# First batch of a two-layer LoRA kernel: another order of VectorE's work around `u_sum`, `h` and the turns of x

## The reference

```
x = x + x @ W0.T + 0.5 * (x @ A0[label]) @ B0.T
x = x + x @ W1.T + bias + 2 * (x @ A1[slot]) @ B1[slot]
```

## Time and profile before

| | |
|---|---|
| timed runs, median (lowest to highest) | 310.39 us (309.81 to 310.56) |
| profiled execution, its own time | 311.65 us |
| its span | 309.8 us |
| mean granted TensorE clock | 0.994 |
| TensorE matmul busy | 300.8 us (97%), 1397 instructions |
| VectorE busy | 233.0 us (75%), 314 |
| ScalarE busy | 139.6 us (45%), 223 |
| GpSimd busy | 68.1 us (22%), 80 |

### The profile page before, as it was taken

How to read it: one execution, slowest core, us unless ns; L and a number is a source line. 1 busy time by engine, 2 the same in 40 slices (tenths; PEclk the granted TensorE clock), 3 DMA queues, 4 the chain that set the end, 5 groups by cost and what they waited for, 6 DMA issues and landing times.

```text
span 309.8 us, 4337 instructions
## 1 busy us (share of the span) xinstructions
PE 300.8 (97%) x1397; PEld 246.1 (79%) x1397; DVE 233.0 (75%) x314; ACT 139.6 (45%) x223; POOL 68.1 (22%) x80
## 2 busy tenths in 40 slices
PE   5999999999999999889999999999999999999995
PEld 4887888888888888578888878878878878878874
DVE  2468997989999999973975975876876876876221
ACT  3556566889348643334254244245245245245010
POOL 4706000010010501520080080080080070070000
PEclk9999999999999999979999999999999999999999
DMA  5999410800006300462283183183093084002012
GB/s 181 293 326 315 49 24 3 129 8 2 0 0 110 62 0 1 65 140 85 37 158 104 29 149 118 22 155 118 16 162 112 17 152 132 11 34 102 0 47 90
DMA packets 99362, 27.55 MB, mean 89 GB/s; under 512 B 84885, under 2 KB 93077, under 8 KB 99350
## 3 DMA queue, kind: packets, MB, share of 16 engines
q1 hardware_dynamic: 99350, 27.41, 37.9%
HBM read 19.01 MB, written 8.39 MB: 88 GB/s over the span
## 4 chain that ended last, share of the span: by engine, by line
PE 79%; DVE 14%; issue 4%; DMA 2%; SPq 0%; ACT 0%; DVEq 0%
PE bank L1026 76%; DVE vt_lo L633 3%; PE bank L1048 2%; DVE xt L855 2%; DVE vt L633 2%; DMA n<-in_L_cond_W 2%; DVE v_lo L633 1%; DVE lhs_lo L633 1%; DVE v L633 1%; DVE s_sum L633 1%; DVE s_lo L633 1%; DVE u_sum L633 0%; DVE z_sum L633 0%; DVE p_lo L633 0%; DVE c_lo L633 0%
## 5 line engine op out<-in xcount | busy, mean ns | idle before, releaser
L1026 PE MATMUL bank<-vt_hi,s_hi 128*128 128x512 f32 x96 | 37.4, 390 | 0.0
L1026 PE MATMUL bank<-vt_lo,s_hi 128*128 128x512 f32 x96 | 37.4, 390 | 0.0
L1026 PE MATMUL bank<-vt_hi,s_lo 128*128 128x512 f32 x96 | 37.3, 389 | 0.0
L855 DVE STREAM_TRANSPOSE xt<-raw 128x512 int32<-128x512 int32 x32 | 32.4, 1082 | 0.0
L417 ACT ACTIVATE lhs_hi<-xt 128x512 fp32r<-128x512 f32 x32 | 19.8, 630 | 25.5 <-PE bank L1026 17.8
L633 DVE TENSOR_TENSOR s_lo<-s_sum,s_hi 128x512 fp32r<-128x512 f32 x32 | 27.6, 886 | 2.9 <-ACT s_hi L417 2.9
L633 DVE TENSOR_TENSOR lhs_lo<-xt,lhs_hi 128x512 fp32r<-128x512 f32 x32 | 24.5, 772 | 4.4 <-ACT lhs_hi L417 4.1
L417 ACT ACTIVATE s_hi<-s_sum 128x512 fp32r<-128x512 f32 x32 | 19.7, 629 | 17.2 <-PE bank L1026 11.0
L377 POOL CAST ac<-c_hi 128x128 fp32r (+1 forms) x8 | 5.7, 707 | 95.1 <-PE bank L1026 86.3
L1026 PE MATMUL bank<-v_lo,lhs_hi 128*128 128x512 f32 x64 | 25.8, 404 | 0.0
L1026 PE MATMUL bank<-v_hi,lhs_lo 128*128 128x512 f32 x64 | 25.0, 391 | 0.0
(11 more groups left out here) (166 smaller groups left out, 753.9 us busy)
## 6 DMA issues: line engine op xcount, KB each, us to landing
raw<-in_x SPq DMA_DIRECT2D x32, 256.0 KB, 4.8
out<-y SPq DMA_DIRECT2D x32, 256.0 KB, 2.1
n<-in_L_cond_W SPq DMA_DIRECT2D x16, 256.0 KB, 6.0
a<-in_L_cond_W SPq DMA_DIRECT2D x16, 256.0 KB, 5.3
a_raw<-in_L_cond_lora_A SPq DMA_DIRECT2D x8, 128.0 KB, 2.4
a_raw<-in_L_cond_lora_As SPq DMA_DIRECT2D x8, 64.0 KB, 2.4
b_raw<-in_L_cond_lora_Bs SPq DMA_DIRECT2D x8, 64.0 KB, 2.0
b_raw<-in_L_cond_lora_B_w SPq DMA_DIRECT2D x1, 128.0 KB, 6.3
```

The costliest lines, as they stand in the source:

```text
L855: nc.vector.transpose(xt[:, n, :, :].rearrange("p e (s sb) -> p sb e s", sb=GR).bitcast(I32), rows[:, n // 2, n % 2].bitcast(I32)).then_in ...
L1026: return nc.tensor.matmul(ps, lhsT, rhs, start=start, stop=stop, skip_group_check=more)
```

## The change

In batch 0 alone VectorE works in another order. Of vt4's four low parts, which stood ahead of the batch, two now stand between `u2_sum` and `u_total`, two behind `u_total`. Quarters 0 and 1 of the next x are turned next; then `z_sum`; then quarter 2; then `h`, which waits for the correction; then z2; then u's low part; then quarter 3, and the low parts of quarter 0, A0 and quarter 2, which stood ahead of and behind `z_sum`. What follows (the low part of sum 0, of quarter 1, the output additions) stays. In the other batches the order is the same as before; `h_and_low` is cut into two functions that stand one behind the other there.

```diff
-            def h_and_low(b):
+            def h_sum(b):
                 dve.wait_ge(corr_done, b + 1)
                 tt(u_sum[32:UB, :], BANK_E[32:UB, 0:S], u_sum[32:UB, :], ALU.add, h_made)
+
+            def u_low(b):
                 dve.wait_ge(u_hi_made, b + 1)
                 tt(u_st[64:64 + UB, :], u_sum[0:UB, :], u_st[0:UB, :].bitcast(F32), ALU.subtract, u_lo_made)
...
-            for m in range(HK):
+
+            def vt4_low(m):
                 dve.wait_ge(vt4_hi_made, m + 1)
                 dve.wait_ge(vt4_made, m + 1)
                 low(vt4_lo, vt4, vt4_hi, m, vt4_lo_made)
...
                 tt(u2_sum[:, :], BANK_B[:, :], m1_sum[:, :], ALU.add, u2_made)
                 if first:
+                    vt4_low(0)
+                    vt4_low(1)
                     dve.wait_ge(zeroed, 4)
                     u_total(b)
+                    vt4_low(2)
+                    vt4_low(3)
                 if not final:
                     dve.wait_ge(s_sum_made, 4 * b + 4)
                     turn_next(b + 1, range(2))
                 if not first:
                     dve.wait_ge(u_lo_made, b)
                     u_total(b)
-                if not final:
-                    turn_next(b + 1, range(2, 4))
-                    a_low(b + 1, 0)
-                    a0_low(b + 1)
+                    if not final:
+                        turn_next(b + 1, range(2, 4))
+                        a_low(b + 1, 0)
+                        a0_low(b + 1)
                 dve.wait_ge(m5_done, b + 1)
                 dve.wait_ge(u2_made, b + 1)
                 if not first:
                     dve.wait_ge(c_made[C22], b)
                 tt(z_sum[:, :], BANK_C[:, :], u2_sum[:, :], ALU.add, z_made)
-                if not final:
+                if first:
+                    turn_next(b + 1, range(2, 3))
+                    h_sum(b)
+                elif not final:
                     a_low(b + 1, 2)
                 dve.wait_ge(m7_done, b + 1)
                 dve.wait_ge(z_made, b + 1)
                 tt(z_sum[:, :], BANK_D[:, :], z_sum[:, :], ALU.add, z2_made)
-                h_and_low(b)
+                if not first:
+                    h_sum(b)
+                u_low(b)
+                if first:
+                    turn_next(b + 1, range(3, 4))
+                    a_low(b + 1, 0)
+                    a0_low(b + 1)
+                    a_low(b + 1, 2)
```

## The result

The changed kernel takes 305.80 us at the median of four runs (305.49 to 306.84), the kernel before 310.48 beside it (309.81 to 310.66). The ratio is 0.9858, with a 95% interval of 0.9832 to 0.9883: 4.4 us less, between 3.6 and 5.2. Forecast were 306.2 us and 4.15 less. The profiled execution took 306.84 us with a span of 305.0 (before: 311.65 and 309.8).

The account below looks back on a forecast made before the run. TensorE's 2.2 us wait for `u_st` in batch 0 was taken as the bound. Profiled 311.65 less 4.15 (2.42 stall, 1.73 slow clock and restart) gives 307.5; timed runs, 1.26 lower, 306.24 us, range 305.6 to 308.2.

Parts of the forecast that it names:

- The hole and its cost: TensorE's wait for `u_st` in batch 0: 2.42 us of stall and 1.73 of slow clock and restart go.
- Up to the turns: VectorE's `u2_sum`, vt4 low parts and `u_total` in batch 0: reordering costs and brings nothing; `u_sum` 0.84 us earlier than needed.
- Turns and h: VectorE in batch 0 finishes turns 0 to 2 and `z_sum` 0.78 us before `h` can start.
- u_low: u's low part in batch 0 takes 0.42 us without GpSimd's sums beside it, 1.07 at the other end.
- All three: Behind the later turn 3: GpSimd's sums, ScalarE's C11 copy and the load of x for batch 2 cost nothing.
- the third sum's chain: Third GpSimd sum through high part, low part and C12 addition: done at 136.1, at worst 138.2, covered by 1.8 us or more.
- The load of x: SyncE's load for batch 2, issued at 130.0, lands by 140.4, at most 141.4; covered by 2.2 to 3.1 us.
- A: Batch 0's hole goes but the clock's share isn't gained in the timed runs: 307.97 us; chance 0.16.
- B: TensorE's wait in batch 0 shrinks but stays, 0.3 to 1 us: 306.5 to 307.2, up to 308.5; chance 0.08.
- C: Turn 3 holds back batch 2's x, so batch 1's turns and TensorE wait: slower, 311.6 us; chance 0.02.
- D: Nothing moves, because a wait other than VectorE's order held `u_low`: 310.4 us; chance 0.02.

Follow-up runs that it names:

- e2: Kernel before, with nine extra matmuls in batch 0 filling TensorE's hole ahead of the wait for u's low part; ratio 0.9961.
- e10: Kernel before, with four extra matmuls in batch 0's hole ahead of the wait for u's low part; ratio 0.9947.
- e1: Kernel before, with only vt4's low parts moved around `u_total`, all else in the old order; ratio 1.0016.
- e3: Changed kernel, with vt4's four low parts back ahead of `u2_sum`, all else in the new order; ratio 0.9895.
- e9: Kernel before, VectorE's order untouched, with GpSimd's sums of batch 0 waiting until u's low part is written; 307.58 us, ratio 0.9903.
- e4: Changed kernel, with the turn of quarter 3 ahead of `h` instead of behind u's low part; ratio 0.9890.
- e6: Changed kernel, with the turn of quarter 3 and all three low parts (quarter 0, A0, quarter 2) ahead of `h`; ratio 0.9923.
- e5: Changed kernel, with the turn of quarter 3 and the low part of quarter 0 ahead of `h`; ratio 0.9898.
- e8: Changed kernel, with x of batch 2 loaded behind batch 0's stores of C11 and C22 instead of ahead; 313.09 us, ratio 1.0078.
- e7: Changed kernel, with the turn of quarter 3 behind the three low parts instead of ahead of them; ratio 0.9889.

## Why the prediction was right

*The hole and its cost.* Forecast 2.42 + 1.73 = 4.15 us, measured 4.16. The split was off by 0.13, since the restart of 0.15 belongs to the stall: e2 and e10 give 1.60 for the clock. The sum took it as paid in every run of the kernel before; by their mean clock 42 of 54 had paid it. The timed median came out 0.4 us under the forecast, which is within the runs' scatter and not explained.

*Up to the turns* cost nothing and brought nothing: shown by e1 and e3.

*Turns and h.* VectorE's slack ahead of `h` was 0.72 (forecast 0.78), `h` 0.64 behind the correction (0.63).

*u_low.* 0.42 us, 0.93 ahead of TensorE (forecast 1.07). The reason given for its length, GpSimd's sums, is shown by e9, but the reading that it is 1.07 "when sums run beside it" was too coarse: e4 to e6 give 0.55, 0.42 and 0.42 with sums about, by how much of a sum was left when it came. The forecast also filed this blocking under margin; e9 shows it to be 1.41 us of the old hole.

*What comes later.* "All three cost nothing" held, but one cover was much thinner than worked out. The step that failed is the first: the third sum's chain "is 136.1, at worst 138.2", covered by 1.8 us. On the changed trace's own scale (0.69 us less) the worst end would be 137.5; C12's addition ended at 139.01 and the cover was 0.33. I had followed the sum through one low part and the addition and left out what stands ahead of them in VectorE's queue: four low parts of 1.50 to 1.79 us and the C22 addition. The load of x was issued at 129.58, 0.3 later than worked out on this scale, and no turn waited for it.

*Rivals.* A fell by the result (3.6 to 5.2 us less, against its 2.42) and by e2 and e10; what stays of it is the quarter of the runs that hadn't paid. B did not come; e5 shows how near it is: 1.5 us more work in front of `h` leaves 0.15 us. C is real as a mechanism, by e8, and did not occur. D fell by the trace.

## What to carry over

When TensorE waits for a short chain through VectorE and ScalarE, look at what stands ahead of the chain in VectorE's fixed order, and put there only as much as fits the time in which the input isn't ready anyway. An idle TensorE costs its idle time and, where the clock falls behind it, more: here 1.6 us on top of 2.56. Where VectorE instructions with two SBUF inputs meet GpSimd's, look at when they meet: moving GpSimd's work by one wait (e9) gave 3 of 4.2 us. When a step is moved back, follow its result through the whole queue of every engine it crosses.

## What the runs showed of the hardware

In the traces the granted clock did not fall in batch 0 behind idle stretches of 0.20 us (e2), 0.70 (e6), 0.86 (e9) and 1.36 (e10). It fell behind 2.25 (the kernel before), 2.36 (e1) and, in batch 1, 3.28 (e8). These are single traces and not a limit, and the same kernel does not do the same each time. By the mean clock of the timed runs it fell in 42 of 54 runs of the kernel before, in 8 of 10 of e1 and in none of the 27 of e2, e9 and e10. One of e6's eight runs had 0.993 and took 308.85 us. One of e3's four, whose trace has no hole in batch 0, had 0.992 and took 308.60 us. For both the place is open; e8's trace shows a low clock, 0.57, in another place too, from 8 to 12 us.

The same front took a different time from run to run: the correction of batch 0 started between 124.92 us (e1) and 127.56 (e10), with nothing changed ahead of it except the place of vt4's low parts. The kept traces say where most of it comes from, the pace of TensorE's first products. Between 8 and 10 us the matmuls of 128x512 start 0.43 us apart in six traces (the kernel before, the changed one, e4, e5, e8, e10), as they do at a granted clock of 0.50 behind the hole, and these have the correction at 126.20 to 127.56. In the other six they start 0.23 apart, and the correction comes at 124.92 to 125.84. In five of the six slow ones the granted clock reads 1.00 there all the same, so its record doesn't show this start. It is a part of the timed runs' scatter that has nothing to do with the change, and the reason why a distance inside the trace tells more here than the span.

A low part of 128x256 took 0.42 us with GpSimd idle (e7) and 1.50 beside GpSimd's sums (changed kernel); a GpSimd copy of 32x16 took 0.19 us beside `h` (changed kernel) and 1.74 beside VectorE's low parts (e6).
